# One product for two sets of group averages, and channel statistics taken earlier, in a fused two-layer image kernel

## The chip, the cores and the metric

The kernel runs on one core of a Trainium2 chip. The metric is the device time of one execution in microseconds (us); the time stated is the median of several executions. The core has TensorE (matrix products, called PE in the profile), VectorE (DVE), ScalarE (ACT), GpSimd (POOL), and SyncE (SP), whose queue issues the DMA transfers. Each engine executes its own instructions in order and waits at semaphores for the others.

## What is computed

The input x holds 32 images of 128 channels and 56x56 pixels. Two layers follow each other, each on a group-normalised input (32 groups of 4 channels) and each added to what went in:

```python
x = x + _L0_conv_ref(_gn(x), ...)   # channel gate: mean per channel -> 3-tap conv with
                                    # fractional offsets -> sigmoid -> x * gate
x = x + _L1_conv_ref(_gn(x), ...)   # key/query/value projections, softmax over 3x3
                                    # neighbours at distances 1, 2 and 4, 1x1 conv out

def _gn(v, G=32, eps=1e-05):
    g = v.reshape(B_, G, C_ // G, H_, W_)
    m = jnp.mean(g, axis=(2, 3, 4), keepdims=True)
    s = jnp.var(g, axis=(2, 3, 4), keepdims=True)
    return ((g - m) / jnp.sqrt(s + eps)).reshape(v.shape)
```

The statistics of the second normalisation follow from those of the first and the gate, so each image is measured once, per channel, and group averages over 4 channels are needed twice: of the channel moments of x (ahead of the gate) and of those of the gated image (behind the gate).

## The kernel before

Channels lie on the 128 partitions. All engines run the same loop: for each image n and each of 25 **slots** t (a slot is one tile of 128 queries of image n), each does its share. A slot lasts 1.2 to 2.4 us, an image 44.73 us. In one slot TensorE computes, in this order: the scores of tile t (`scores`, L473), the transposes of tile t-3 (`transposed`, L487), in some slots the hidden layer of a strip (`hidden`, L527) or value products (`values`, L553), the context of tile t-5 (`context`, L508 and L513), in some slots the second layer of the strip one slot behind (`query_and_key`, L534), and last a product of the chain of statistics (`chain`).

VectorE in a slot: `masked` (L1036, reads the scores and finds their extreme), `reciprocals` and `scaled` for tile t-1 (L1044, L1053 or L1050), then `chain` (statistics L1092 and small steps), then `final` (L1061) or `values` (L1074). ScalarE: copies transposed tiles (L667), `exponentials` of tile t (L652), which wait for VectorE's `masked` of the same tile, and, except for strips 0 and 3, `hidden` (L675) only behind the exponentials; then keys (L697) and queries (L686). TensorE's `query_and_key` waits for `hidden` of ScalarE (semaphore `h_done`). Slots of hidden layers are `G_SLOT`; strip 4 has its hidden layer in slot 5 and its L534 in slot 6.

The **chain** of an image m (the gate and both normalisations) runs ahead of the image, at places given in the table `CH` and counted from two images ahead: place 25+t is slot t of image m-1, place t is slot t of image m-2. It has these steps: `STATS`: seven `bn_stats` (L1092), one for each seventh of the image; `aggr`: `bn_aggr` into `of_x` (L1097); `p1`: one small GpSimd step (L811); `c1`: TensorE's product with `group_avg` into the bank `ps_v`, 6 columns (L569); `d1`: VectorE copies them out to `in_x` and squares them (L1100, L1101); `p3` to `p7` with `c3`: the gate; `c4`: a second product with `group_avg`, of the gated moments `of_x1`, 6 columns (L576); `d9`: copy to `in_x1` and squares (L1136, L1137); `p11`, `pw`, `c6`, `d13`: scaled weights and bias for the image.

The bank `ps_v` is also where the value products of seven column blocks go (`V_SLOT`, slots 4, 7, 10, 17, 18, 21 and 24). So `values` on TensorE waits (semaphore `dg`, table `CHAIN_READS`) until VectorE has copied out what the chain left there. `c4` stands at place 28, at the end of slot 3; the next value product is in slot 4.

In the order of every queue the tables alone decide: nothing is rescheduled at run time. The load of image n+3 (`LOAD`) stands in slot 19.

Of the kernel before, what the change touches and what calls it, by code (L numbers as in the profile page):

```python
# [19 lines left out]
GN = 4  # L20
# [34 lines left out]
CH = dict(aggr=12, p1=12, c1=13, d1=14, p3=15, c3=19, d4=20, a4=21, p4=21, d6=25,  # L55
          a6=25, d7=26, p7=26, c4=28, d9=28, p11=31, pw=32, c6=36, d13=37)
# [141 lines left out]
def build(nc, x, par, w1, w2, wv, wo, bo, bv, wg, out):  # L198
    with ExitStack() as ctx:
# [66 lines left out]
        of_x = sb("of_x", [P, 2 + GN])  # L266
        of_x1 = sb("of_x1", [P, 2 + GN])
        in_x = sb("in_x", [P, 2 + GN])
        in_x1 = sb("in_x1", [P, 2 + GN])
# [111 lines left out]
        def images(first, last, drain=0, register=None):  # L381

            with nc.Block() as block:
# [73 lines left out]
                def _(pe):  # L457
# [79 lines left out]
                    def values(m, b):  # L537
# [19 lines left out]
                    def chain(m, at):  # L557
                        if at in (ch(m)["c1"], ch(m)["c3"], ch(m)["c4"], ch(m)["c6"]):
# [650 lines left out]
```

## Time and profile before

| | us |
|---|---|
| median of 3 runs | 1479.59 |
| lowest, highest | 1479.5, 1479.63 |
| profiled execution | 1480.63 |
| its span | 1478.9 |

| engine | busy us | share of the span |
|---|---|---|
| PE | 1445.5 | 98% |
| PE weight loads | 1180.4 | 80% |
| DVE | 1256.4 | 85% |
| ACT | 1169.7 | 79% |
| POOL | 914.7 | 62% |

All times of rows are from this one execution, counted from the start of its span. Ends of matmuls are modelled, so the distance from one start to the next is the better measure of what an instruction costs. A fp32 product is listed as two (x2). The mean granted clock of TensorE is 0.997.

### The profile page before, as it was taken

The numbers are of one execution on the slowest core, as the hardware profiler recorded it, in microseconds if no ns is written. First come the engines' busy times: TensorE is split into PE (matmuls) and PEld (weight loads), VectorE is DVE, ScalarE is ACT, GpSimd is POOL, SyncE is SP. The second block draws the span as 40 slices with busy tenths as digits, with TensorE's granted clock in tenths as the row PEclk, the third lists the DMA queues.
The fourth block names the chain that finished last, engine by engine and source line by source line (L and its number), as shares of the span: only waits on it lengthen the run. The fifth ranks groups of instructions, "written<-read, shape, count | busy, mean of one in ns | idle before, by whom it ended". The sixth has DMA issues, their size and how long they took to land.

```text
span 1478.9 us, 34970 instructions
## 1 busy us (share of the span) xinstructions
PE 1445.5 (98%) x9123; PEld 1180.4 (80%) x9123; DVE 1256.4 (85%) x4602; ACT 1169.7 (79%) x3047; POOL 914.7 (62%) x2049
## 2 busy tenths in 40 slices
PE   5899999999999999999999999999999999999998
PEld 2688888888888888888888888888888888888886
DVE  7788888888888888888888888888888888888876
ACT  3688888788878788778788778888878888787886
POOL 5766566576666575665675665665665765665730
PEclk9999999999999999999999999999999999999999
DMA  3334554445554345554345554445544455544344
GB/s 137 86 95 151 171 154 127 119 144 154 161 163 127 110 144 163 155 166 117 113 148 167 155 156 109 128 151 170 155 127 122 140 154 164 161 127 112 101 117 145
DMA packets 104706, 205.95 MB, mean 139 GB/s; under 512 B 13632, under 2 KB 83776, under 8 KB 96448
## 3 DMA queue, kind: packets, MB, share of 16 engines
q1 hardware_dynamic: 103632, 203.49, 46.4%
q8 instruction: 79, 1.29, 0.4%
q14 instruction: 115, 0.94, 0.2%
q10 hardware_dynamic: 880, 0.23, 0.1%
HBM read 51.62 MB, written 51.38 MB: 70 GB/s over the span
## 4 chain that ended last, share of the span: by engine, by line
PE 96%; issue 1%; POOL 1%; ACT 0%; DVE 0%; ACTq 0%; POOLq 0%; DVEq 0%
PE ps_s L473 24%; PE ps_o L508 20%; PE ps_v L553 12%; PE ps_t L487 12%; PE ps_p L527 11%; PE ps_p L534 11%; PE ps_o L513 3%; PE ps_v L573 0%; PE ps_v L576 0%; PE ps_v L569 0%; PE ps_v L580 0%; PE ps_t L534 0%; ACT qq L686 0%; POOL hats L831 0%; ACT hid L675 0%
## 5 line engine op out<-in xcount | busy, mean ns | idle before, releaser
L652 ACT ACTIVATE e<-e,zmin 128x256 f32<-128x256 f32 x800 | 403.1, 504 | 154.4 <-DVE zmin L1036 150.6
L1036 DVE CUSTOM_DVE_ANT_0 e<-ps_s,mask 128x256 f32<-128x256 f32 x800 | 337.3, 422 | 146.8 <-PE ps_s L473 138.6
L508 PEld LDWEIGHTS ps_o<-eT,v 128*128 128x128 f32 x2688 | 380.3, 191 | 82.9 <-issue 70.2
L508 PE MATMUL ps_o<-eT,v 128*128 128x128 f32 x2688 | 430.3, 275 | 0.4 <-ACT eT L667 0.3
L473 PE MATMUL ps_s<-kk,qq 128*128 128x256 f32 x1408 | 427.6, 386 | 1.7 <-DVE zmin L1036 1.7
L897 POOL TENSOR_SCALAR xb<-raw,g 128x32 f32<-128x32 f32 (+3 forms) x768 | 353.8, 476 | 0.0
L487 PE MATMUL ps_t<-ident,e 128*128 128x128 f32 x1600 | 305.7, 273 | 0.0
L487 PEld LDWEIGHTS ps_t<-ident,e 128*128 128x128 f32 x1600 | 225.2, 141 | 80.5 <-issue 0.2
L667 ACT ACTIVATE eT<-ps_t 128x512 f32<-128x512 f32 (+1 forms) x416 | 236.8, 569 | 63.9 <-PE ps_t L487 60.5
L1053 DVE SCALAR_TENSOR_TENSOR e<-e,rz,keep 128x256 f32<-128x256 f32 x480 | 254.6, 530 | 17.1
L473 PEld LDWEIGHTS ps_s<-kk,qq 128*128 128x128 f32 x1408 | 223.6, 192 | 49.0 <-issue 40.5
L553 PE MATMUL ps_v<-wvoT,xb 128*128 128x128 f32 x1580 | 214.7, 276 | 3.8 <-issue 0.2
L527 PE MATMUL ps_p<-raw,w1x 128*128 128x448 f32 x448 | 207.7, 545 | 1.1 <-ACT hid L675 0.7
L534 PE MATMUL ps_p<-hid,w2T 128*128 128x448 f32 x442 | 203.9, 543 | 1.8 <-ACT hid L675 1.8
L553 PEld LDWEIGHTS ps_v<-wvoT,xb 128*128 128x128 f32 x1580 | 193.8, 192 | 10.4 <-issue 10.4
L686 ACT ACTIVATE qq<-ps_p,bn_t 64x192 f32<-64x192 f32 x442 | 195.0, 441 | 7.6
L870 POOL TENSOR_SCALAR raw<-raw,g 128x448 f32<-128x448 f32 x224 | 175.8, 789 | 33.2 <-PE ps_p L527 33.2
L697 ACT ACTIVATE kk<-ps_p,bn_t 64x448 f32<-64x448 f32 x221 | 139.5, 631 | 36.0 <-PE ps_p L534 23.5
L652 ACT ACTIVATION_READ_ACCUMULATOR e<-e,zmin 128x1 f32 x800 | 150.9, 189 | 0.0
L675 ACT ACTIVATE hid<-ps_p,b1x 128x448 f32<-128x448 f32 x224 | 140.5, 627 | 12.3 <-PE ps_p L527 8.8
L1050 DVE TENSOR_SCALAR e<-e,rz 128x256 f32<-128x256 f32 x320 | 134.1, 419 | 11.4
L1061 DVE TENSOR_TENSOR raw<-raw,ps_o 128x448 f32<-128x448 f32 x224 | 137.6, 614 | 3.8 <-PE ps_o L513 1.7
(150 smaller groups left out, 1550.9 us busy)
## 6 DMA issues: line engine op xcount, KB each, us to landing
out_dram<-raw SPq DMA_DIRECT2D x32, 1568.0 KB, 5.7
raw<-in_x_dram SPq DMA_DIRECT2D x31, 1568.0 KB, 6.6
v<-v SPq DMA_DIRECT2D x192, 224.0 KB, 2.9
kk<-kk SPq DMA_DIRECT2D x192, 112.0 KB, 2.2
ksp<-kk SPq DMA_DIRECT2D x192, 64.0 KB, 2.1
v<-v_last SPq DMA_DIRECT2D x64, 128.0 KB, 2.9
kk<-kk SPq DMA_DIRECT2D x32, 224.0 KB, 2.9
v<-v_last SPq DMA_DIRECT2D x64, 96.0 KB, 2.7
```

The lines of the kernel that those rows point to most:

```text
L473: nc.tensor.matmul(ps_s[i][:, 0:KEYS].rearrange("p (s h k) -> p h s k", s=2, h=2), qq[:, t, :], window.rearrange("p h (s k) -> p h s k", s=2),
L487: last = nc.tensor.transpose(o[:, base:base + KEYS].rearrange("p (a s k) -> p s a k", a=2, s=2)[:, i], e[:, t % RING, P * i:P * (i + 1)], ...
L508: last = nc.tensor.matmul(o[:, UPIX * (u - 1):UPIX * (u + 1)], v[:, s, u, :], eT[:, UPIX * (base + 2 * u - 1):UPIX * (base + 2 * u + 1)], ...
L527: nc.tensor.matmul(ps_p[:, 0:SPIX].rearrange("p (r c) -> p r c", c=SIDE), w1x[:, m.parity(), :], strip_of(m, g), start=True, stop=True).th ...
L534: nc.tensor.matmul(qk_bank(m, g)[:, 0:SPIX], w2T[:], hid[:], start=True, stop=True).then_inc(qk_ps.next(), 1)
L553: last = nc.tensor.matmul(v_bank(m, b)[:, P * j:P * (j + 1)], pixels, wvoT[:], start=True, stop=True)
L652: nc.scalar.activation(e[:, i, :], e[:, i, :], ACT.Exp, bias=zmin[:, i:i + 1], scale=-1.0, accum_out=zs[:, i:i + 1]).then_inc(e_done.next( ...
L667: nc.scalar.activation(eT[:, base:base + size], ps_t[(EPAIRS * n.parity() + j) % 2][:, 0:size], ACT.Copy).then_inc(eT_done.next(), 1)
L686: last = nc.scalar.activation(qq[HD * b:HD * (b + 1), at:at + len(units), UPIX * b:UPIX * (b + 1)], src[:, units[0]:UNITS:2, :], ACT.Relu, ...
L897: last = gp.tensor_scalar(to[:, k, rs, cs], src, col(Y_A + m.parity()), col(Y_B + m.parity()), ALU.mult, ALU.add)
L1036: nc.vector.tensor_tensor_reduce(e[:, i, :], ps_s[(TILES * n.parity() + t) % 2][:, 0:KEYS], mask[:].rearrange("p s h a b -> p (s h a b)"), ...
L1053: nc.vector.scalar_tensor_tensor(e[:, i, :], e[:, i, :], rz[:, i:i + 1], keep[:, KINDS.index(outside(t)), :], ALU.mult, ALU.mult).then_inc ...
```

## The change

For images 2 to 31 the product `c1` is gone. The moments of image m+1 ahead of its gate and those of image m behind its gate lie side by side in one buffer (`moments`), and `c4` of image m multiplies all 12 columns at once; one copy brings all 12 out (`averages`), and two squaring steps follow, one for each image. Images 0 and 1 (`alone`) keep a `c1` of their own. Since the moments of image m+1 must be ready by then, its statistics come earlier: `STATS` goes from slots 22 | 2, 4, 6, 8, 10, 11 to slots 22, 23, 24 | 0, 2, 3, 4, `aggr` and `p1` from slot 12 to slot 5. `c4` and `d9` go from place 28 (slot 3) to place 31 (slot 6), `p11` from 31 to 33, `pw` from 32 to 34. `LOAD` goes from 19 to 18.

```diff
-CH = dict(aggr=12, p1=12, c1=13, d1=14, p3=15, c3=19, d4=20, a4=21, p4=21, d6=25,
-          a6=25, d7=26, p7=26, c4=28, d9=28, p11=31, pw=32, c6=36, d13=37)
+CH = dict(aggr=5, p1=5, c1=6, d1=6, p3=15, c3=19, d4=20, a4=21, p4=21, d6=25,
+          a6=25, d7=26, p7=26, c4=31, d9=31, p11=33, pw=34, c6=36, d13=37)
...
-STATS = {-3: (0,), 2: (1,), 4: (2,), 6: (3,), 8: (4,), 10: (5,), 11: (6,)}
-
-LOAD = 19
+STATS_0 = {-3: (0,), 2: (1,), 4: (2,), 6: (3,), 8: (4,), 10: (5,), 11: (6,)}
+STATS = {-3: (0,), -2: (1,), -1: (2,), 0: (3,), 2: (4,), 3: (5,), 4: (6,)}
+
+LOAD = 18
...
-CHAIN_READS = ((2, "d1"), (4, "d4"), (13, "d9"), (15, "d13"))
-N_DG, N_PG, N_CG, N_AG = 15, 32, 4, 4
+CHAIN_READS = ((1, "d4"), (10, "d9"), (12, "d13"))
+N_DG, N_PG, N_CG, N_AG = 12, 31, 2, 4
+MOMENTS = 6
...
+def alone(m):
+
+    return m.offset < 2
...
+        def columns(m):
+
+            return 2 * MOMENTS if (m + 1).exists() and not alone(m + 1) else MOMENTS
...
-                        if at == ch(m)["c1"]:
+                        if at == ch(m)["c1"] and alone(m):
...
                         if at == ch(m)["c4"]:
-                            pe.wait_ge(pg.sem, pg.count(m, 21))
-                            nc.tensor.matmul(ps_v[:, 0:2 + GN], group_avg[:], of_x1[:], start=True,
-                                             stop=True).then_inc(cg.next(), 1)
+                            pe.wait_ge(pg.sem, pg.count(m, 20))
+                            if columns(m) > MOMENTS:
+                                pe.wait_ge(da.sem, da.count(m + 1, 1))
+                                pe.wait_ge(pa.sem, pa.count(m + 1, 1))
+                            nc.tensor.matmul(ps_v[:, 0:columns(m)], group_avg[:], moments[:, m.parity(), 0:columns(m)],
+                                             start=True, stop=True).then_inc(cm.next(), 1)
...
                         if at == ch(m)["d9"]:
-                            dve.wait_ge(cg.sem, cg.count(m, 3))
-                            step(13, nc.vector.tensor_copy(in_x1[:], ps_v[:, 0:2 + GN]))
-                            step(14, nc.vector.scalar_tensor_tensor(squares[:], moment(in_x1, APART, GN), 1.0,
-                                                                    moment(in_x1, APART, GN), ALU.mult, ALU.mult,
+                            dve.wait_ge(cm.sem, cm.count(m, 1))
+                            step(10, nc.vector.tensor_copy(averages[:, m.parity(), 0:columns(m)], ps_v[:, 0:columns(m)]))
+                            step(11, nc.vector.scalar_tensor_tensor(squares[:], moment(in_x1(m), APART, GN), 1.0,
+                                                                    moment(in_x1(m), APART, GN), ALU.mult, ALU.mult,
                                                                     accum_out=col(SQ1)))
+                            if columns(m) > MOMENTS:
+                                square_x(m + 1, 2)
```

How rows move, at three places. In these listings an instruction stands with its line, its tiles (`g` is a table of single columns, `ps_...` are PSUM banks) and the semaphores that it waits for; lines of the changed kernel are some 30 higher.

**TensorE, end of slot 3 and slot 4.** Before, from the context products of slot 3 to the value products of slot 4:

```order
L508 MATMUL ps_o<-eT,v 128x128 [waits eT_done]
L508 MATMUL ps_o<-eT,v 128x128
L576 MATMUL ps_v<-of_x,group_avg 128x6 [waits pg,v_done]
L473 MATMUL ps_s<-kk,qq 128x2x2x64 [waits q_done,z_done,k_copied1,k_copied0]
L487 MATMUL ps_t<-ident,e 128x2x64 [waits n_done]
L487 MATMUL ps_t<-ident,e 128x2x64
L553 MATMUL ps_v<-wvoT,xb 128x128 [waits dg,xb_done,v_done]
L553 MATMUL ps_v<-wvoT,xb 128x128 x3
```

Now, the same stretch:

```order
L535 MATMUL ps_o<-eT,v 128x128 [waits eT_done]
L535 MATMUL ps_o<-eT,v 128x128
L500 MATMUL ps_s<-kk,qq 128x2x2x64 [waits q_done,z_done,k_copied1,k_copied0]
L514 MATMUL ps_t<-ident,e 128x2x64 [waits n_done]
L514 MATMUL ps_t<-ident,e 128x2x64
L582 MATMUL ps_v<-wvoT,xb 128x128 [waits dg,xb_done,v_done]
L582 MATMUL ps_v<-wvoT,xb 128x128 x3
```

The 6-column product that stood between slot 3 and the scores of slot 4 is gone, and the value product L553 (now L582) no longer has a chain product shortly ahead of it.

**TensorE, end of slot 6 and slot 7.** Before, from the context products of slot 6 to the value products of slot 7:

```order
L508 MATMUL ps_o<-eT,v 128x128 [waits eT_done]
L508 MATMUL ps_o<-eT,v 128x128
L534 MATMUL ps_p<-hid,w2T 128x448 [waits h_done]
L473 MATMUL ps_s<-kk,qq 128x2x2x64 [waits q_done,z_done,k_copied0,k_copied1]
L487 MATMUL ps_t<-ident,e 128x2x64 [waits eT_done,n_done]
L487 MATMUL ps_t<-ident,e 128x2x64
L553 MATMUL ps_v<-wvoT,xb 128x128 [waits dg,xb_done,v_done]
```

Now, the same stretch:

```order
L535 MATMUL ps_o<-eT,v 128x128 [waits eT_done]
L535 MATMUL ps_o<-eT,v 128x128
L561 MATMUL ps_p<-hid,w2T 128x448 [waits h_done]
L610 MATMUL ps_v<-moments,group_avg 128x12 [waits da,pa,pg,v_done]
L500 MATMUL ps_s<-kk,qq 128x2x2x64 [waits q_done,z_done,k_copied0,k_copied1]
L514 MATMUL ps_t<-ident,e 128x2x64 [waits eT_done,n_done]
L514 MATMUL ps_t<-ident,e 128x2x64
L582 MATMUL ps_v<-wvoT,xb 128x128 [waits dg,xb_done,v_done]
```

The 12-column product stands now behind L534 (now L561) of slot 6, ahead of the value product of slot 7, and waits for the moments of the next image too (`da`, `pa`).

**VectorE, slots 2 to 4** (`ISA e,zmin` is `masked`). Before, from `scaled` in slot 2 to `masked` in slot 4:

```order
L1053 SCALAR_TENSOR_TENSOR e<-e,rz,keep 128x256 [waits rz_done]
L1092 BN_STATS stats<-raw 128x6
L1036 ISA e,zmin<-ps_s,mask 128x256 [waits e_done,t_done,s_done]
L1036 ISA zmin 128x1
L1044 RECIPROCAL rz<-zs 128x1 [waits e_done]
L1053 SCALAR_TENSOR_TENSOR e<-e,rz,keep 128x256 [waits rz_done]
L1136 COPY in_x<-ps_v 128x6 [waits cg]
L1137 SCALAR_TENSOR_TENSOR squares,g<-in_x 128x4 [waits dg]
L1036 ISA e,zmin<-ps_s,mask 128x256 [waits t_done,e_done,s_done,dg]
```

Now, the same engine from `scaled` in slot 3 to `values` in slot 4:

```order
L1087 SCALAR_TENSOR_TENSOR e<-e,rz,keep 128x256 [waits rz_done]
L1133 BN_STATS stats<-raw 128x6
L1070 ISA e,zmin<-ps_s,mask 128x256 [waits e_done,t_done,s_done]
L1070 ISA zmin 128x1
L1078 RECIPROCAL rz<-zs 128x1 [waits e_done]
L1087 SCALAR_TENSOR_TENSOR e<-e,rz,keep 128x256 [waits rz_done]
L1133 BN_STATS stats<-raw 128x6
L1108 TENSOR_TENSOR v<-ps_v,wobv 128x512 [waits c_done,v_ps]
```

The copy and the squares are gone from slot 3, and a `bn_stats` (now L1133) stands there; the copy with its two squares is in slot 6 now. In slots 23, 24 and 0, which these rows don't show, one `bn_stats` each is new in the same way, and the ones of slots 6, 8, 10 and 11 are gone. The order of ScalarE's instructions and that of SyncE's transfers are the same in both kernels: between slots 18 and 19 SyncE has nothing else.

## Rows read from the trace of the kernel before

**Rows 1.** The page: busy time by engine, and the chain that ended last.

```profile
PE 1445.5 (98%) x9123; PEld 1180.4 (80%) x9123; DVE 1256.4 (85%) x4602; ACT 1169.7 (79%) x3047; POOL 914.7 (62%) x2049
...
PE 96%; issue 1%; POOL 1%; ACT 0%; DVE 0%; ACTq 0%; POOLq 0%; DVEq 0%
```

**Rows 2.** Timeline of TensorE, slot 13 twice; columns: start us, length us, instruction, count.

```profile
696.80 0.28 PE L569 MATMUL ps_v<-of_x,group_avg 128*128 128x6 f32 x2
...
741.53 0.28 PE L569 MATMUL ps_v<-of_x,group_avg 128*128 128x6 f32 x2
...
742.19 0.38 PE L487 MATMUL ps_t<-ident,e 128*128 128x128 f32 x2
```

**Rows 3.** Timeline of TensorE: value products of slot 17, and slots 3 and 4.

```profile
702.59 1.06 PE L553 MATMUL ps_v<-wvoT,xb 128*128 128x128 f32 x8
...
722.98 0.28 PE L576 MATMUL ps_v<-of_x,group_avg 128*128 128x6 f32 x2
...
723.64 0.38 PE L487 MATMUL ps_t<-ident,e 128*128 128x128 f32 x2
724.15 1.13 PE L553 MATMUL ps_v<-wvoT,xb 128*128 128x128 f32 x8
```

**Rows 4.** Waits over the whole span: us in total, times, longest us.

```profile
PEld ps_v L553 <- issue: 10.4, 32, 0.4
```

**Rows 5.** Timeline of VectorE, slot 23 to the start of slot 5, same image.

```profile
714.10 0.42 DVE L1036 CUSTOM_DVE_ANT_0 e<-ps_s,mask 128x256 f32<-128x256 f32 x1 [0.28 <-PE ps_s L473]
...
715.95 0.42 DVE L1036 CUSTOM_DVE_ANT_0 e<-ps_s,mask 128x256 f32<-128x256 f32 x1 [0.29 <-PE ps_s L473]
...
717.72 0.42 DVE L1036 CUSTOM_DVE_ANT_0 e<-ps_s,mask 128x256 f32<-128x256 f32 x1 [0.27 <-PE ps_s L473]
...
718.26 0.70 DVE L1053 SCALAR_TENSOR_TENSOR e<-e,rz,keep 128x256 f32<-128x256 f32 x1
...
721.62 0.48 DVE L1053 SCALAR_TENSOR_TENSOR e<-e,rz,keep 128x256 f32<-128x256 f32 x1
722.02 0.62 DVE L1092 BATCH_NORM_STATS2 stats<-raw 128x6 f32<-128x448 f32 x1
722.55 0.41 DVE L1036 CUSTOM_DVE_ANT_0 e<-ps_s,mask 128x256 f32<-128x256 f32 x1
...
723.08 0.74 DVE L1053 SCALAR_TENSOR_TENSOR e<-e,rz,keep 128x256 f32<-128x256 f32 x1
723.75 0.15 DVE L1136 COPY in_x<-ps_v 128x6 f32<-128x6 f32 x1
...
724.47 0.42 DVE L1036 CUSTOM_DVE_ANT_0 e<-ps_s,mask 128x256 f32<-128x256 f32 x1
...
726.54 0.42 DVE L1036 CUSTOM_DVE_ANT_0 e<-ps_s,mask 128x256 f32<-128x256 f32 x1
```

**Rows 6.** Timeline of ScalarE, slot 5.

```profile
727.00 0.51 ACT L652 ACTIVATE e<-e,zmin 128x256 f32<-128x256 f32 x1 [1.36 <-DVE zmin L1036]
...
727.50 0.61 ACT L675 ACTIVATE hid<-ps_p,b1x 128x448 f32<-128x448 f32 x1
```

**Rows 7.** Timeline of TensorE, slot 6.

```profile
727.19 0.60 PE L473 MATMUL ps_s<-kk,qq 128*128 128x256 f32 x2
727.62 0.38 PE L487 MATMUL ps_t<-ident,e 128*128 128x128 f32 x2
727.84 0.61 PE L508 MATMUL ps_o<-eT,v 128*128 128x128 f32 x4
728.29 0.92 PE L534 MATMUL ps_p<-hid,w2T 128*128 128x448 f32 x2
```

**Rows 8.** Timelines of ScalarE and TensorE, same pair of lines, slot 6 of image 0.

```profile
55.61 0.61 ACT L675 ACTIVATE hid<-ps_p,b1x 128x448 f32<-128x448 f32 x1
...
56.28 1.02 PE L534 MATMUL ps_p<-hid,w2T 128*128 128x448 f32 x2 [0.43 <-ACT hid L675]
```

**Rows 9.** Timeline of GpSimd, slots 2 and 3.

```profile
722.84 1.58 POOL L870 TENSOR_SCALAR raw<-raw,g 128x448 f32<-128x448 f32 x2
```

More of the change, by code:

```diff
@@ L265, in build @@
         spread_s = sb("spread_s", [P, GN])
[L266 to L269, printed above, removed]
+        moments = sb("moments", [P, 2, 2 * MOMENTS])
+        averages = sb("averages", [P, 2, 2 * MOMENTS])
         squares = sb("squares", [P, GN])
@@ L307, in build, with of_x1, of_x, in_x1 @@
         N_BAND = N_IOTA + 3 + 4
+        def of_x1(m):
+            return moments[:, m.parity(), 0:MOMENTS]
+        def of_x(m):
+            return moments[:, (m + 1).parity(), MOMENTS:2 * MOMENTS]
+        def in_x1(m):
+            return averages[:, m.parity(), 0:MOMENTS]
+        def in_x(m):
+            return averages[:, (m + 1).parity(), MOMENTS:2 * MOMENTS]
+        def columns(m):
+            return 2 * MOMENTS if (m + 1).exists() and not alone(m + 1) else MOMENTS
         def qk_bank(m, g):
@@ L548, in values @@
                                 pe.wait_ge(dg.sem, dg.count(m + 1, max(held, default=0)))
+                                if alone(m + 1) and ch(m + 1)["d1"] <= V_SLOT[b] + TILES:
+                                    pe.wait_ge(da.sem, da.count(m + 1, 2))
                             held = [k for k, at in CHAIN_READS if ch(m)[at] <= V_SLOT[b] + 2 * TILES]
@@ L557, in chain @@
                     def chain(m, at):
-                        if at in (ch(m)["c1"], ch(m)["c3"], ch(m)["c4"], ch(m)["c6"]):
+                        if at in (ch(m)["c3"], ch(m)["c4"], ch(m)["c6"]) or at == ch(m)["c1"] and alone(m):
                             banks = sum(v_at <= at - TILES for v_at in V_SLOT)
@@ L584, in tables @@
                     def tables(t):
[L585 removed]
+                        if t == FIRST["c1"] + 1:
                             pe.wait_ge(g_const, N_ID)
@@ L903, in slot @@
                             chain(m, at)
-                        if n.offset == first + 1 and t == CH["p3"] + 1:
+                        if n.offset == first + 1 and t == FIRST["p3"] + 1:
                             borders()
@@ L1076, in values, with square_x @@
                                                 ALU.add).then_inc(v_done.next(), 1)
+                    def square_x(m, counts):
+                        nc.vector.scalar_tensor_tensor(squares[:], moment(in_x(m), APART, GN), 1.0,
+                                                       moment(in_x(m), APART, GN), ALU.mult, ALU.mult,
+                                                       accum_out=col(SQ)).then_inc(da.next(counts), counts)
+                        dve.wait_ge(da.sem, da.count(m, 3))
                     def chain(m, at):
@@ L1082, in step @@
                             dve.wait_ge(dg.sem, dg.count(m, k))
-                        for u in (STATS_1 if m.offset == 1 else STATS).get(at, ()):
+                        for u in {0: STATS_0, 1: STATS_1}.get(m.offset, STATS).get(at, ()):
                             if u == (2 * (PIECES - 1) if m.offset == 0 else 0):
@@ L1095, in chain @@
                             dve.wait_ge(bs_done.sem, bs_done.count(m, UNITS))
[L1096 to L1106 removed]
+                            nc.vector.bn_aggr(moment(of_x(m), MEAN, 2), stats[:].rearrange("p a b -> p (a b)")
+                                              ).then_inc(da.next(), 1)
+                        if at == ch(m)["d1"] and alone(m):
+                            dve.wait_ge(c_alone, m.offset + 1)
+                            nc.vector.tensor_copy(in_x(m), ps_v[:, 0:MOMENTS]).then_inc(da.next(), 1)
+                            dve.wait_ge(da.sem, da.count(m, 2))
+                            square_x(m, 1)
+                        if at == ch(m)["d4"]:
+                            dve.wait_ge(cg.sem, cg.count(m, 1))
+                            step(1, nc.vector.tensor_copy(pooled_row[:], ps_v[:, 8:8 + P]))
                             dve.wait_ge(ag.sem, ag.count(m + -1, 3))
```

123 lines of the change are left out of this document (58 added, 65 removed).

## The prediction

> **What bounds the kernel now.** The page first: TensorE is busy 98% of the span and carries 96% of the chain that ended last [rows 1]. So nothing counts that doesn't take work from TensorE or make it wait. The next view is TensorE's timeline over one image in the middle. The product c1 of two successive images starts at 696.80 and 741.53 [rows 2]: an image takes 44.73 us. In it I went from each product's start to the next, looking for a distance above what the same kind costs elsewhere, and found one. The transposes of a slot cost 0.22 us (727.62 to 727.84) [rows 7], but from those of slot 4 (723.64) to the value products (724.15) it is 0.51 [rows 3]: a gap of 0.29 us. It recurs in every image: the loads of weights ahead of L553 sat idle 32 times for 10.4 us in all [rows 4]. VectorE's timeline shows why. The value products wait until d9 has copied the averages out of the shared bank, and the copy starts at 723.75 only, because the `scaled` ahead of it took 0.74 us [rows 5].
>
> Third, how close is each other wait of TensorE to being late? The closest is L534 of slot 6. It waits for `hidden` on ScalarE, which stands behind the exponentials of slot 5, which wait for `masked` of slot 5 on VectorE. These start at 726.54, 727.00 and 727.50 [rows 5, 6], L534 at 728.29 [rows 7]. Where L534 was seen waiting for that line, it started 0.67 us after `hidden` did (55.61 to 56.28) [rows 8]. So it could have started at 727.50 + 0.67 = 728.17: 0.12 us to spare. That is what I watch for any delay of VectorE.
>
> **What is taken from TensorE.** From c1's start to the next transposes it is 0.66 us (741.53 to 742.19), for the scores alone 0.43 (727.19 to 727.62) [rows 2, 7]: c1 costs 0.23 us. The widened c4 costs what it did: four products of 128 columns are listed at 1.06 in slot 17, 0.27 each, and c4 with 6 columns at 0.28 [rows 3], so 6 columns more are 0.00, at most 0.01. It leaves slot 3 and comes back in slot 6, behind L534. The gap of 0.29 goes, since no product of the chain stands ahead of slot 4's value products any more, and with it the slower start behind a wait: L553 is listed at 1.13 there and at 1.06 in slot 17, 0.07 us [rows 3]. If nothing became late, each image would gain 0.23 + 0.29 + 0.07 = 0.59 us, and 30 images 17.7 us.
>
> **What is added to VectorE ahead of slot 5.** From slot 23 to slot 4 VectorE had one `bn_stats` in slot 2 and one in slot 4; now it has them in 23, 24, 0, 2, 3 and 4, four more. Each takes 0.53 us from its start to the next start (722.02 to 722.55): + 2.12 us. The copy and the square of slot 3 go, 723.75 to 724.47: - 0.72. Before, `masked` of slot 5 began 726.54 - 714.10 = 12.44 us after that of slot 23, and in these 12.44 us VectorE waited only twice, 0.29 and 0.27 us, ahead of slots 24 and 0. An instruction with a follower right behind it gives way 0.08 us earlier than listed (0.62 against those 0.53 or 0.54), so the slack is 0.29 + 0.27 + 0.16 = 0.72 us, and it is used up: - 0.72. One more term: `scaled` took 0.70 us in slot 0 (718.26) and 0.74 in slot 3 (723.08), against 0.48 in slot 2 (721.62) [rows 5]. The one of slot 3 began 0.24 us into a step L870 of GpSimd [rows 9]. In slot 0 VectorE will be some 0.3 us later than GpSimd, past most of such a step, so - 0.22. In slot 3 I keep the long one, since GpSimd's two L870 stand behind a reciprocal of VectorE in slot 1 and are as late as VectorE itself. The sum: 12.44 + 2.12 - 0.72 - 0.72 - 0.22 = 12.90 us. Nothing changes for TensorE and VectorE before slot 23, so `masked` of slot 5 begins at 714.10 + 12.90 = 727.00 in place of 726.54.
>
> **What is late next.** L534 of slot 6 can start at 727.00 + 0.96 (726.54 to 727.50) + 0.67 = 728.63. TensorE would be ready for it at 728.29 - 0.59 = 727.70, as c4, the gap and the slow start are gone ahead of it. It waits 0.93 us, and behind a wait L534 is listed at 1.02 in place of 0.92: another 0.10 [rows 7, 8]. Behind L534 stands c4 (0.23) now, where c1 (0.23) was further on, which cancels. An image gets longer by 728.63 + 0.10 - 728.29 = **0.44 us**: a gain of 0.59 is paid for with 1.03.
>
> **Other terms, each with its cover.** c4 waits for GpSimd's p1 of the next image, which follows `bn_aggr` in VectorE's slot 5, about 1.2 us after `masked` of that slot; TensorE comes to c4 2.4 us after it, since it stands behind the same VectorE: 0. The value products of slot 7 wait for d9 again. VectorE will be through with `scaled` of slot 6 and wait for c4. It can begin the copy some 0.40 behind c4's start and TensorE can go on 0.40 behind the copy's start (723.75 to 724.15 [rows 3, 5]), 0.80 in all; TensorE gets there 0.88 behind c4 (0.66 and the transposes' 0.22 [rows 2, 7]). So 0, with 0.08 to spare. The second square stands behind the copy, where slots 8, 10 and 11 have lost their statistics, and can't cost more than the 0.72 that copy and square took together. Keys and queries on ScalarE come 0.6 us later in slots 2 and 3, about 0.2 us before slot 5's hidden layer needs them: 0. GpSimd's p11 and pw come two slots later, two slots before their readers. The order of transfers and of ScalarE is the same: 0.
>
> **The sum.** 29 images x 0.44 = 12.8 us. The next to last image has no statistics to take ahead and only gains, - 0.37, and once c1 goes with no c4 behind L534 in its place, - 0.23. At the start VectorE also gets more to do; I take 0, within 1 us either way. The span becomes 1478.9 + 12.2 = 1491.1 us. The profiled execution took 1480.63 around a span of 1478.9, and the median of the runs is 1479.59, 0.69 above the span. By the median the forecast is **1491.8 us**.
>
> **Its own bounds.** If `scaled` of slot 3 meets no step of GpSimd, 0.26 less per image: 1484.3 us. If those of slots 0 and 4 meet one too, 0.22 each: 0.44 more per image, 1504.6 us.
>
> **Rival 1: VectorE keeps up, and the kernel is faster.** All of 17.7 us comes: 1461.9 us. For this `masked` of slot 5 must begin at 727.70 - 0.96 - 0.67 = 726.07 or earlier, 0.93 before my value. For it speaks VectorE's 85% on the page, that is, 15% idle; against it, that of this idle time only 0.72 us lie between slots 23 and 5. Chance 0.10. **Rival 2: gain and wait cancel**, which an error of 0.44 us in those 12.90 would do: 1479.6 us. Chance 0.09.
>
> **Rival 3: GpSimd's steps shut VectorE out for longer.** In slot 3 `scaled` began within the first L870 (722.84; two in 1.58, so the first ended at 723.63), and VectorE's next instruction began at 723.75, 0.12 behind that end [rows 5, 9]. If instead `scaled` ran whole behind GpSimd's step, 0.40 (722.02 less 721.62), slot 3 would take 0.28 more: 0.28 x 29 = 8 us, 1499.9 us. The condition is that VectorE's later place meets GpSimd's steps less luckily than in the rows. The Trainium skill (SBUF — State Buffer, section "SBUF: two separate sides") states as a rule that GpSimd and a VectorE instruction with two SBUF inputs contend for one pair of ports, that the first gets it for its whole instruction, and that the other fully blocks. By that rule the time would be this rival's; the rows agree that something is held back until L870 ends, but show 0.12 and not 0.40 behind it. Chance 0.14.
>
> **Rival 4: the second copy is late too.** If in slot 7 VectorE is busy when c4 is done, the value products lose there what they lost in slot 4, 0.29 + 0.07 per image, 10.4 us: 1502.2 us. It decides at 0.08 us of delay. Against it: by the sum VectorE is through with `scaled` of slot 6 some 0.3 us before c4's result. Chance 0.12.
>
> **How the numbers follow.** Forecast 0.55, rivals 0.10, 0.09, 0.14 and 0.12. The range of eight in ten leaves out rivals 1 and 2 and the far end of the bounds: 1483 to 1506. A change of 0.2% (3 us) is about the least that can be told from none. Faster by more than that 0.11, within it 0.10, slower by more 0.79.
>
> **What would show it.** Right: in the trace after, TensorE has no gap ahead of the value products of slot 4 and one near 0.93 us ahead of L561 (the old L534) in slot 6, ended by ScalarE's `hidden`; ScalarE's exponentials of slot 5 wait for VectorE; VectorE has no idle time from slot 23 to slot 5; an image takes 45.17 us. Wrong: no gap in slot 6 and an image of 44.14 us (rival 1, and with it the sum on VectorE), a `scaled` of 1 us in slot 3 (rival 3), a second gap ahead of the value products of slot 7 (rival 4).

## The result, and the profile after

| | before | after |
|---|---|---|
| median of 4 runs each, us | 1479.61 | 1495.26 |
| lowest, highest | 1479.5, 1480.65 | 1494.73, 1495.92 |
| profiled execution, us | 1480.63 | 1494.73 |
| its span | 1478.9 | 1493.0 |

The ratio of the times is 1.0101, with a 95% interval of 1.0089 to 1.0113: the change costs 1%, 15.65 us by the medians and 14.1 us by the two profiled executions. The mean granted clock of TensorE is 0.996 (0.997 before). Forecast were +12.2 us and 1491.8 us.

The page of the changed kernel, first the busy times, then the chain that ended last; VectorE has entered it with 2%, ScalarE with 2% [rows 1 has both at 0%]:

```profile
PE 1440.2 (96%) x9063; PEld 1175.4 (79%) x9063; DVE 1234.3 (83%) x4572; ACT 1167.1 (78%) x3047; POOL 918.2 (62%) x2049
...
PE 92%; ACT 2%; DVE 2%; issue 1%; DMA 1%; POOL 0%; SPq 0%; ACTq 0%; DVEq 0%; POOLq 0%
```

Waits of TensorE and of its weight loads over the span (us in total, times, longest). There is one new wait, at strip 4's second layer, once in nearly every image; first its row before, then after. The loads ahead of the value products are down from 10.4 us in 32 times [rows 4] to 0.4 in 2.

```profile
PE ps_p L534 <- ACT hid L675: 1.8, 2, 1.3
```

```profile
PE ps_p L561 <- ACT hid L709: 23.4, 31, 1.0
...
PEld ps_v L582 <- issue: 0.4, 2, 0.2
```

TensorE's timeline from slot 4 to slot 7, which answers to [rows 3] and [rows 7]:

```profile
687.13 0.38 PE L514 MATMUL ps_t<-ident,e 128*128 128x128 f32 x2
687.34 1.06 PE L582 MATMUL ps_v<-wvoT,xb 128*128 128x128 f32 x8
...
690.96 0.61 PE L535 MATMUL ps_o<-eT,v 128*128 128x128 f32 x4
692.37 1.02 PE L561 MATMUL ps_p<-hid,w2T 128*128 128x448 f32 x2 [0.80 <-ACT hid L709]
693.22 0.29 PE L610 MATMUL ps_v<-moments,group_avg 128*128 128x12 f32 x2
693.36 0.68 PE L500 MATMUL ps_s<-kk,qq 128*128 128x256 f32 x2
693.88 0.38 PE L514 MATMUL ps_t<-ident,e 128*128 128x128 f32 x2
694.10 0.83 PE L582 MATMUL ps_v<-wvoT,xb 128*128 128x128 f32 x6
```

From the transposes of slot 4 to the value products it is 0.21 us, where it was 0.51. L561 follows the context products by 1.41 us where L534 followed them by 0.45 (727.84 to 728.29): 0.96 of waiting. The value products of slot 7 come 0.88 behind L610, with no gap.

VectorE's timeline, the same image, answers to [rows 5]; ScalarE's to [rows 6]:

```profile
677.81 0.42 DVE L1070 CUSTOM_DVE_ANT_0 e<-ps_s,mask 128x256 f32<-128x256 f32 x1 [0.28 <-PE ps_s L500]
...
682.28 0.48 DVE L1087 SCALAR_TENSOR_TENSOR e<-e,rz,keep 128x256 f32<-128x256 f32 x1
...
687.40 0.74 DVE L1087 SCALAR_TENSOR_TENSOR e<-e,rz,keep 128x256 f32<-128x256 f32 x1
688.07 0.61 DVE L1133 BATCH_NORM_STATS2 stats<-raw 128x6 f32<-128x448 f32 x1
...
689.12 0.57 DVE L1087 SCALAR_TENSOR_TENSOR e<-e,rz,keep 128x256 f32<-128x256 f32 x1
...
690.75 0.41 DVE L1070 CUSTOM_DVE_ANT_0 e<-ps_s,mask 128x256 f32<-128x256 f32 x1
...
693.55 0.17 DVE L1176 COPY averages<-ps_v 128x12 f32<-128x12 f32 x1 [0.39 <-PE ps_v L610]
```

```profile
691.20 0.51 ACT L686 ACTIVATE e<-e,zmin 128x256 f32<-128x256 f32 x1 [1.24 <-DVE zmin L1070]
...
691.70 0.61 ACT L709 ACTIVATE hid<-ps_p,b1x 128x448 f32<-128x448 f32 x1
```

`masked` of slot 5 starts 690.75 - 677.81 = 12.94 us after that of slot 23, and the rest of the chain follows as before: exponentials 0.45, hidden layer 0.50, L561 0.67 us later. Between these two no wait of VectorE is listed. From one L561 of slot 6 to the next it is 45.10 or 45.11 us in most images, where before it was 44.72 or 44.73: +0.38.

**Where the 14.1 us are.** I followed that one product of slot 6 through both traces:

| stretch, to the product of slot 6 | before | after | difference |
|---|---|---|---|
| start of the span to image 0 | 56.28 | 58.15 | +1.87 |
| image 0 to 1 | 45.87 | 46.52 | +0.65 |
| image 1 to 29, 28 intervals | 1252.31 | 1264.35 | +12.04 |
| 29 to 30 | 44.71 | 44.15 | -0.56 |
| 30 to 31 | 43.59 | 43.85 | +0.26 |
| 31 to the end of the span | 36.14 | 35.98 | -0.16 |

Of the 12.04, 28 x 0.38 = 10.6 are the regular images and 1.4 a few irregular ones, the longest 45.82 and 45.70. Image 1 is regular too: its L561 waits 0.80 us, as in the images behind it. So 0.38 of the 0.65 is the ordinary growth of an image, 29 x 0.38 = 11.0 in all, and the start proper costs 1.87 + 0.27 = 2.1 us.

### The profile page after: what moved, and what is told of

It is laid out like the page before. It is cut to its first block, busy times and chain, and to the rows that moved or that the text cites. A ratio compares the mean times of both kernels' runs of the same rounds, so it can differ in the third digit from the quotient of the medians.

```text
span 1493.0 us, 34698 instructions
## 1 busy us (share of the span) xinstructions
PE 1440.2 (96%) x9063; PEld 1175.4 (79%) x9063; DVE 1234.3 (83%) x4572; ACT 1167.1 (78%) x3047; POOL 918.2 (62%) x2049
## 4 chain that ended last, share of the span: by engine, by line
PE 92%; ACT 2%; DVE 2%; issue 1%; DMA 1%; POOL 0%; SPq 0%; ACTq 0%; DVEq 0%; POOLq 0%
PE ps_s L500 23%; PE ps_o L535 19%; PE ps_v L582 12%; PE ps_p L561 11%; PE ps_t L514 11%; PE ps_p L554 11%; PE ps_o L540 3%; ACT hid L709 1%; DMA ksp<-kk 1%; DVE stats L1133 1%; PE ps_v L604 0%; ACT e L686 0%; DVE e L1070 0%; DVE v L1108 0%; PE ps_s L637 0%
## 5 line engine op out<-in xcount | busy, mean ns | idle before, releaser
L931 POOL TENSOR_SCALAR xb<-raw,g 128x32 f32<-128x32 f32 (+3 forms) x768 | 362.0, 486 | 0.0
L1087 DVE SCALAR_TENSOR_TENSOR e<-e,rz,keep 128x256 f32<-128x256 f32 x480 | 243.2, 507 | 17.1
L561 PE MATMUL ps_p<-hid,w2T 128*128 128x448 f32 x442 | 207.0, 550 | 23.4 <-ACT hid L709 23.4
L582 PE MATMUL ps_v<-wvoT,xb 128*128 128x128 f32 x1580 | 213.4, 276 | 0.0
L582 PEld LDWEIGHTS ps_v<-wvoT,xb 128*128 128x128 f32 x1580 | 194.4, 192 | 0.4 <-issue 0.4
L864 POOL TENSOR_SCALAR hats<-hats 128x128 f32<-128x128 f32 x93 | 32.8, 353 | 249.0 <-ACT hats L757 243.5
L904 POOL TENSOR_SCALAR raw<-raw,g 128x448 f32<-128x448 f32 x224 | 166.9, 750 | 29.8 <-PE ps_p L554 29.6
L1084 DVE TENSOR_SCALAR e<-e,rz 128x256 f32<-128x256 f32 x320 | 140.0, 438 | 11.4
```

What stands on the lines that cost most here:

```text
L561: nc.tensor.matmul(qk_bank(m, g)[:, 0:SPIX], w2T[:], hid[:], start=True, stop=True).then_inc(qk_ps.next(), 1)
L582: last = nc.tensor.matmul(v_bank(m, b)[:, P * j:P * (j + 1)], pixels, wvoT[:], start=True, stop=True)
L931: last = gp.tensor_scalar(to[:, k, rs, cs], src, col(Y_A + m.parity()), col(Y_B + m.parity()), ALU.mult, ALU.add)
L1087: nc.vector.scalar_tensor_tensor(e[:, i, :], e[:, i, :], rz[:, i:i + 1], keep[:, KINDS.index(outside(t)), :], ALU.mult, ALU.mult).then_inc ...
```

## The experiments

Each kernel's time stands against runs of the kernel before on the same chip (1479.6 to 1480.8 us). "An image" is the distance that most images have in the trace. The three theories on trial: that VectorE's four more `bn_stats` ahead of slot 5 make strip 4's hidden layer late (mine); that c4's wait for the next image's moments holds TensorE; that what was taken off TensorE was worth less than I summed.

**e1: the hidden layer of strip 4 ahead of the exponentials, in the changed kernel.**

```diff
-RELU_FIRST = (0, 3)
+RELU_FIRST = (0, 3, 4)
```

> The changed kernel, with one more entry in ScalarE's table of strips whose hidden layer comes ahead of the slot's exponentials: strip 4 (slot 5). Theory (the statistics make VectorE late, and the lateness reaches TensorE only through the exponentials ahead of strip 4's hidden layer): the gap of 0.8 us ahead of L561 in slot 6 goes, an image takes 44.14 instead of 45.11 us, 29 images x 0.96 = 28 us less: 1467 us. Rival (the loss comes from c4 in its new place, from GpSimd or from transfers): 1490 us or more, since none of these is touched.

Measured 1479.97 us (10 runs), ratio to before 0.9995 [0.9985, 1.0004]; an image 44.56 us. The wait of L561 is gone, and with it 15 us. But the 1467 us were missed, and the rival's 1490 too: another wait had stood behind it. Timelines of e1, TensorE, VectorE, GpSimd:

```profile
686.00 0.92 PE L561 MATMUL ps_p<-hid,w2T 128*128 128x448 f32 x2
687.03 0.36 PE L610 MATMUL ps_v<-moments,group_avg 128*128 128x12 f32 x2
...
688.08 0.91 PE L582 MATMUL ps_v<-wvoT,xb 128*128 128x128 f32 x6
```

```profile
686.14 0.34 DVE L1137 BATCH_NORM_AGGREGATE moments<-stats 128x2 f32<-128x42 f32 x1
```

```profile
686.58 0.31 POOL L845 TENSOR_SCALAR moments<-spread_s,moments 128x4 f32<-128x4 f32 x1 [1.74 <-DVE moments L1137]
```

L610 starts 1.03 behind L561, where 0.75 is what that product takes without a wait (e3, below: 678.59 to 679.34): 0.28 late for `bn_aggr` and p1. It runs slowly behind the wait, and the value products of slot 7 are late too (688.08, 1.05 behind L610 in place of 0.88). So the second theory holds as well, but only once the first wait is out of the way. Five images took 45.04 to 45.30 us; in each a product waits for a transfer of keys, 3 us in all.

**e2: the same edit in the kernel before.**

> The same entry in the kernel before. Theory: there that wait had 0.12 us to spare and was never late, so nothing comes of it: 1479.6 us, within 1 us. Rival (the order on ScalarE is worth something by itself): 1470 us or less, and then e1 says little about the statistics.

1480.41 us, 1.0002 [0.9992, 1.0011]: nothing, as expected. e1's gain is a wait undone, not a better order as such.

**e3: the kernel before with only c4 moved**, from slot 3 to slot 6, behind L534, and with it the steps that read its result.

```diff
-a6=25, d7=26, p7=26, c4=28, d9=28, p11=31, pw=32, c6=36, d13=37)
+a6=25, d7=26, p7=26, c4=31, d9=31, p11=33, pw=34, c6=36, d13=37)
...
```

> The kernel before with c4, d9, p11 and pw at the places of the changed kernel (31, 31, 33, 34), c1 kept, the statistics where they were. Theory: the gap ahead of slot 4's value products and the slow start behind it go, 0.36 us x 30 images = 10.8 us less, 1468.8 us; no gap ahead of L534, since VectorE loses 0.72 us ahead of slot 5 and gains nothing. Rival (c4 behind L534 makes slot 7's value products wait as they did in slot 4): 1479.6 us.

1470.21 us, 0.9926 [0.991, 0.9943]; an image 44.35 us, -0.37. TensorE's timeline of e3, slots 6 and 7:

```profile
678.59 0.92 PE L534 MATMUL ps_p<-hid,w2T 128*128 128x448 f32 x2
679.34 0.28 PE L576 MATMUL ps_v<-of_x,group_avg 128*128 128x6 f32 x2
679.48 0.68 PE L473 MATMUL ps_s<-kk,qq 128*128 128x256 f32 x2
680.00 0.38 PE L487 MATMUL ps_t<-ident,e 128*128 128x128 f32 x2
680.22 0.83 PE L553 MATMUL ps_v<-wvoT,xb 128*128 128x128 f32 x6
```

That is the gap of 0.29 and the slow start of 0.07, as summed, and the value products of slot 7 don't wait (0.88 behind c4). One part of the change is a gain by itself.

**e4: the kernel before with only the statistics moved** to the changed kernel's slots.

> The kernel before with only the statistics moved to slots 22, 23, 24, 0, 2, 3 and 4 (bn_aggr stays in slot 12, both products and all else as before). Theory: masked of slot 5 comes 12.44 + 2.12 - 0.72 = 13.84 us behind that of slot 23, or 0.22 less, since slot 3 keeps its copy and squares; L534 then starts 1.06 to 1.28 us later and costs 0.10 more, 1.16 to 1.38 us per image x 29 = 34 to 40 us more, plus 1 to 2 at the start: 1514 to 1521 us. Rival (statistics may stand anywhere, VectorE is 15% idle): 1479.6 us.

1514.65 us, 1.0231 [1.0216, 1.0247], an image 45.83 us, 1.11 more than before, just under the 1.16 to 1.38 expected. TensorE waits at both places where it depends on VectorE:

```profile
PE ps_v L554 <- DVE in_x L1137: 16.0, 29, 0.6
...
PE ps_p L535 <- ACT hid L676: 8.5, 31, 1.3
```

The statistics alone cost 34 us; the rest of the change, c4 and d9 moved and c1 gone, gives 19 of them back.

**e5: the changed kernel with four statistics at half size** (`bn_stats` 1, 2, 3 and 5 of images 2 to 31 read 224 columns; the variances are those of part of the image).

```diff
-nc.vector.bn_stats(stats[:, u, :], raw[:, m.offset % RAWS, first:first + BATCH]
+size = BATCH // 2 if m.offset > 1 and u in (1, 2, 3, 5) else BATCH
+nc.vector.bn_stats(stats[:, u, :], raw[:, m.offset % RAWS, first:first + size]
```

> The changed kernel, but the four statistics of slots 23, 24, 0 and 3 read 224 columns in place of 448 (so the statistics of images from the third on are of part of their columns). Nothing else changes on any engine. Theory (VectorE's load ahead of slot 5 is the cause): each is 0.23 us shorter; two of them then fit into the waits that VectorE had ahead of slots 24 and 0, so masked of slot 5 comes 0.6 to 0.8 us earlier, the wait ahead of L561 falls from 0.97 to 0.15 to 0.35 us, an image takes 44.3 to 44.5 us: 1472 to 1478 us. Rival (not VectorE's load, but c4 and what surrounds it): 1495 us.

1475.03 us, 0.9966 [0.9953, 0.9978], an image 44.45 us; the wait of L561 for `hid` is down from 23.4 us to 6.1. It follows VectorE's time.

**e7: e1 and e5 together.**

> e1 and e5 together: hidden of strip 4 first, and four statistics of half the columns. In e1 a gap of 0.28 us ahead of c4 and one of 0.10 ahead of slot 7's value products were left. Theory (c4 waits there for bn_aggr and p1, which are late with VectorE): with VectorE 0.6 us earlier both go, an image takes 44.14 us against 44.56 in e1, 12 us less than e1: 1467 to 1469 us. Rival (c4 waits for something of its own, such as GpSimd's order): as e1, 1480 us.

1463.45 us, 0.9885 [0.987, 0.99], under the 1467 to 1469 expected; an image 44.03 us, and neither L561 nor L610 waits in the middle of the run. This is what an image costs TensorE, and it is 0.70 under 44.73, while I had summed 0.59. The rest is a gap of before that I had not seen (its timeline, slot 15):

```profile
743.29 0.38 PE L487 MATMUL ps_t<-ident,e 128*128 128x128 f32 x2
743.54 0.99 PE L527 MATMUL ps_p<-raw,w1x 128*128 128x448 f32 x2
744.36 0.39 PE L508 MATMUL ps_o<-eT,v 128*128 128x128 f32 x2
```

The hidden layer's product starts 0.25 behind the transposes in place of 0.22 and takes 0.82 to the next start in place of 0.75: 0.03 and a slow start of 0.07, 0.10 us in each image. In e7 the same product starts 0.22 behind and takes 0.75. In the kernel before it starts 0.1 us behind the end of ScalarE's queries (742.54 + 0.90), which it must wait for. The gap stands in the four kernels that keep `bn_aggr` in slot 12 and `d1` in slot 14 (before, e2, e3, e4) and in none of the others. e8 has a product in slot 13 again and doesn't have it, so it isn't c1's time on TensorE; which of the other two makes the queries late no run separates. The third theory falls: what was taken away was worth more than I had said.

**e8: the changed kernel with a product of 6 columns put back into slot 13.**

```diff
+if at == 13 and not alone(m):
...
+    nc.tensor.matmul(ps_v[:, 200:206], group_avg[:], group_avg[:, 0:6], start=True, stop=True)
```

> The changed kernel with a product of 6 columns put back where c1 stood, at the end of slot 13, of tables into unused columns of ps_v; nobody reads it. It measures c1's price by itself. By the rows of before 0.23 us x 30 = 6.9 us more: 1502.2 us. Rival (so small a product hides in the weight loads of its neighbours): 1495.3 us.

1498.43 us, 1.0119 [1.0104, 1.0134] against the changed kernel's 1.0101: +3.2 us in place of +6.9. In the trace an image is 45.27 or 45.32, +0.16 to +0.22, and the product delays its successors by 0.23, of which part is taken back ahead of L561, which waits for VectorE anyway. Another 1.3 us of the difference are the slow images of the changed kernel (1.4 us, see above), of which e8's trace has next to none. The price of c1, 0.23, holds up to the next wait; that it holds for the whole time these runs can't show, as their intervals are as wide as the difference.

**e10: image 2 as before too**, its own c1 in slot 13 and its statistics in the old slots, images 3 to 31 as in the change.

```diff
-    return m.offset < 2
+    return m.offset < 3
...
+         2: dict(CH, aggr=12, p1=12, c1=13, d1=14)}
...
-{0: STATS_0, 1: STATS_1}.get(m.offset, STATS)
+{0: STATS_0, 1: STATS_1, 2: STATS_0}.get(m.offset, STATS)
```

> The changed kernel with image 2 as before too: its own c1 in slot 13 of image 1 and its statistics in the old slots; images 3 to 31 as in the change. Theory: the 2.5 us that the changed kernel loses in images 0 and 1 (its L561 of slot 6 of image 0 starts 1.9 us later than before, that of image 1 another 0.65) come from image 2's statistics, taken while VectorE is late at the start, and from c4 of image 1, which waits for p1 of image 2. Then these 2.5 us come back, less 0.23 for the c1: that line starts near 56.3 us in image 0 and 102.2 in image 1, and the whole time is 2 us under the changed kernel's, 1492 to 1494 us. Rival: the start is lost to something else (the order of first loads, LOAD in slot 18), and the first L561 of slot 6 stays near 58 us, 1495 us.

1493.74 us, 1.0087 [1.0072, 1.0102]. The product of slot 6 is at 56.70 in image 0 and 102.82 in image 1 (58.15 and 104.67 after, 56.28 and 102.15 before). So 1.85 of the 2.5 us come back: most of the start is image 2's statistics, taken in image 0 while TensorE waits for VectorE anyway, and c4 of image 1 that waits for p1 of image 2; the run doesn't separate the two. 0.67 us stay. By their size they are image 1's ordinary growth, 0.38 (its L561 waits 0.79 here too), and image 2's own c1, 0.23. What is left is less than two executions differ by over this stretch: e8, the same kernel up to there, has that product of image 0 at 57.71, the changed kernel at 58.15. So this result rests on the two traces; the whole times, 1.0087 and 1.0101, have overlapping intervals.

**Better places.** Three more kernels keep the one product of 12 columns and e1's order on ScalarE, and give the statistics more room by a later c4; a fourth, e11, takes e1's order away again.

e6, with c4 and d9 in slot 9:

```diff
-CH = dict(aggr=5, p1=5, c1=6, d1=6, p3=15, c3=19, d4=20, a4=21, p4=21, d6=25,
-          a6=25, d7=26, p7=26, c4=31, d9=31, p11=33, pw=34, c6=36, d13=37)
+CH = dict(aggr=8, p1=8, c1=6, d1=6, p3=15, c3=19, d4=20, a4=21, p4=21, d6=25,
+          a6=25, d7=26, p7=26, c4=34, d9=34, p11=35, pw=36, c6=38, d13=39)
...
-STATS = {-3: (0,), -2: (1,), -1: (2,), 0: (3,), 2: (4,), 3: (5,), 4: (6,)}
+STATS = {-3: (0,), 0: (1,), 2: (2,), 3: (3,), 5: (4,), 6: (5,), 8: (6,)}
...
```

> The changed kernel with strip 4's hidden layer ahead of the exponentials (as in e1), and c4 and d9 three slots later still, in slot 9 ahead of the value products of slot 10; so the statistics need to be ready only by slot 8 and stand in slots 22, 0, 2, 3, 5, 6 and 8, bn_aggr and p1 in slot 8, p11, pw, c6 and d13 at 35, 36, 38 and 39. Theory (both waits that e1 and the changed kernel show come from VectorE being late from statistics that lie close together): neither c4 nor L561 nor slot 10's value products wait, an image takes 44.14 us, 0.59 less than before, 1462 to 1465 us. Rival (one product for two sets can't be fed in time wherever it stands, GpSimd's p11 then being late for c6 and the blocks of slot 11): 1480 us or more.

1470.84 us, 0.9932 [0.9917, 0.9947]: no better than e3, and neither the theory's time nor the rival's. Most images take 44.37 to 44.48, some 0.4 more than in e7. TensorE loses it in three places: 0.10 at the hidden layer's product of slot 8 (see e9), 0.11 at the value products of slot 21 and 0.19 at the second layer's product of slot 23. The value products of slot 21 wait for the copy d4 of slot 20, behind a `scaled` (a TENSOR_SCALAR there) that takes 0.91 us where e7 has 0.35. That slot 23 is late from the same cause is argued, not shown. VectorE and GpSimd in e6:

```profile
969.68 0.91 DVE L1084 TENSOR_SCALAR e<-e,rz 128x256 f32<-128x256 f32 x1
970.51 0.27 DVE L1146 COPY pooled_row<-ps_v 128x128 f32<-128x128 f32 x1
```

```profile
967.72 2.72 POOL L931 TENSOR_SCALAR xb<-raw,g 128x32 f32<-128x32 f32 x6
```

`scaled` gives way only where GpSimd's run of six copies ends, 970.44. It began 0.24 us into the fifth of them (969.44 to 969.80) and stood through the whole sixth (969.79 to 970.45). The same two in e7:

```profile
965.03 0.35 DVE L1084 TENSOR_SCALAR e<-e,rz 128x256 f32<-128x256 f32 x1
```

```profile
958.52 2.83 POOL L931 TENSOR_SCALAR xb<-raw,g 128x32 f32<-128x32 f32 x6
```

There the run was over at 961.35, two slots before: a later c4 makes w1x late, and all copies behind it.

e9, with c4 in slot 8 (place 33, everything else of the chain one slot sooner than in e6), in two forms: a with statistics in slots 22 | 0, 2, 3, 5, 6, 7, b in 22, 23 | 0, 2, 3, 5, 6.

> The changed kernel with the hidden layer of strip 4 ahead of the exponentials on ScalarE, the 12-column product and its copy in slot 8 (place 33), bn_aggr and p1 in slot 7, and the statistics in slots 22, 0, 2, 3, 5, 6, 7. Slot 8 has no value products, and those of slot 10 come two slots behind the copy. In e6, with the product in slot 9, an image took 44.4 us in place of the 44.03 seen without a wait; the trace there shows VectorE's scaled of slot 20 at 0.91 us in place of 0.35, ending where a run of six edge copies of GpSimd (L931) ends, and the value products behind it late. Theory: the product in slot 9 made w1x and with it these copies late; one slot sooner they are 1.8 us earlier and miss that scaled: image 44.03 to 44.15 us, 1458 to 1464 us. Rival: some scaled is met all the same, image 44.3 to 44.5, 1467 to 1473 us.

> As e9_c4_33a, with the statistics in slots 22, 23, 0, 2, 3, 5, 6, so that bn_aggr has a slot without a bn_stats. Theory: the same as e9_c4_33a within 3 us, if VectorE has room in slot 23; rival: the bn_stats in slot 23 makes VectorE late at slot 5 again, with L561 waiting, and the image 0.1 to 0.5 us longer than in e9_c4_33a.

a: 1463.45 us, 0.9884 [0.987, 0.9899]; b: 1466.82 us, 0.9907 [0.989, 0.9923]. In a that `scaled` is 0.35 again, since the six copies end 0.40 before it; slot 18's is met instead (0.77), where nobody waits. Both lags of slots 21 and 23 are gone. VectorE and GpSimd of e9 a:

```profile
960.92 0.77 DVE L1087 SCALAR_TENSOR_TENSOR e<-e,rz,keep 128x256 f32<-128x256 f32 x1
...
964.76 0.35 DVE L1084 TENSOR_SCALAR e<-e,rz 128x256 f32<-128x256 f32 x1
```

```profile
961.39 2.97 POOL L931 TENSOR_SCALAR xb<-raw,g 128x32 f32<-128x32 f32 x6
```

An image takes 44.16 or 44.22 us, slightly over the 44.03 to 44.15 expected. All that is left above e7's 44.03 lies in one place, slot 8. There the hidden layer's product waits for ScalarE's queries of the strip before and starts slowly; TensorE and ScalarE of e9 a:

```profile
677.10 0.38 PE L514 MATMUL ps_t<-ident,e 128*128 128x128 f32 x2
677.40 1.02 PE L554 MATMUL ps_p<-raw,w1x 128*128 128x448 f32 x2
678.26 0.38 PE L535 MATMUL ps_o<-eT,v 128*128 128x128 f32 x2
```

```profile
676.46 0.90 ACT L720 ACTIVATE qq<-ps_p,bn_t 64x256 f32<-64x256 f32 x2
```

It starts 0.30 behind the transposes in place of 0.22 and takes 0.86 to the next start in place of 0.75. With c4 gone from slot 6 TensorE comes to it 0.22 us sooner than in e7: once more a wait that stood behind another one.

**Form a is the best full kernel of this study, 1.2% under the one before**, with the same work. In b most images take 44.14 to 44.21, so the `bn_stats` in slot 23 does no harm; its 3.4 us over a (within 3 was expected) lie in five images of 44.6 to 45.3, where TensorE waits for a transfer:

```profile
PE ps_s L500 <- DMA ksp<-kk: 2.7, 5, 0.8
```

e11, form a with strip 4's hidden layer behind the exponentials again:

> e9_c4_33a with the hidden layer of strip 4 behind the exponentials again, as in before and after. Theory: VectorE has one bn_stats more than before between slots 23 and 5 (0.53 us) and the copy and square less (0.72), so masked of slot 5 comes at most 0.2 us sooner than before, while TensorE comes to L561 of slot 6 0.69 us sooner; with 0.12 us to spare before it waits 0.4 us and starts slowly, 0.10: an image of 44.6 to 44.7 us, 1475 to 1479 us. Rival: moving the later statistics was enough and L561 doesn't wait, an image of 44.2 us, 1462 to 1465 us.

1471.17 us, 0.9933 [0.9916, 0.995], an image 44.42 or 44.49; L561 waits 0.1 to 0.2 us and starts slowly. Theory (1475 to 1479) and rival (1462 to 1465) were both missed. The direction is that of the theory, the size is not: I had taken 0.4 of waiting. From `masked` of slot 23 to that of slot 5 it is 12.32 us there, 0.12 less than before.

## Why the prediction was right, and where its sizes were off

**What bounds it, and what is late next: shown.** The gap of slot 4 went; L561 of slot 6 took its place as the wait, by the chain named: VectorE's `masked`, exponentials, hidden layer. 12.94 us between the two `masked` against 12.90 forecast; 1.62 us from `masked` to L561 against 1.63; 0.96 of waiting against 0.93. e1 (the wait taken away) and e5 (VectorE's work halved) moved the time as the chain says, and e4 shows that it is the statistics.

**The sum on VectorE: right in its parts, too.** `scaled` of slot 0 took 0.48, as assumed, that of slot 3 0.74, as assumed. That of slot 4 took 0.57 in place of 0.48, as it met one of GpSimd's small copies: slot 4 came out 0.08 longer than summed, the other slots 0.04 shorter in all.

**What is taken from TensorE: mis-sized**, 0.59 in place of 0.70 (e7). The step that failed is the search for distances above what the same kind costs elsewhere: the prediction names one and there are two. The second, in slot 15, is 0.10 in all. So an image grew by 0.38 and not by 0.44: over 29 images 1.7 us less than forecast.

**The start: "0 within 1 us" was wrong**, +2.1 beside image 1's ordinary growth. The term was put at nothing without a reason. Image 0 isn't like the others: TensorE waits for VectorE in it, and an argument from a middle image says nothing about that. The wait for ScalarE's hidden layer [rows 8] and one for GpSimd's chain were already in the trace of before. The last chain product of that stretch, behind slot 6 of image 0, waits twice as long now, and for another step: before for p7 of its own image (L848), now for p1 of image 2 (L845). First the row of before, then that of after:

```profile
57.84 0.36 PE L576 MATMUL ps_v<-of_x,group_avg 128*128 128x6 f32 x2 [0.54 <-POOL of_x L848]
```

```profile
60.30 0.36 PE L610 MATMUL ps_v<-moments,group_avg 128*128 128x12 f32 x2 [1.13 <-POOL moments L845]
```

e10 brings 1.85 back, and in it this product waits 0.53 us for p7 again.

**Transfers at 0: 1.4 us in a few images.** In the longest, TensorE waits for the copies of keys:

```profile
427.62 0.70 PE L500 MATMUL ps_s<-ksp,qq 128*128 128x256 f32 x2 [0.46 <-DMA ksp<-kk]
```

Weight loads waited 7.6 us for them, 1.4 before, and all four images of 45.25 us or more have such a wait. It comes and goes from trace to trace (0.7 in e9 a, 6.7 in e9 b, 2.1 in e8, which is nearly the changed kernel). With one trace of each kernel no run tells whether the arrangement or the execution sets it: it stays open.

**c4's wait at 0: right only behind the other wait.** I gave as cover that TensorE "stands behind the same VectorE", and so it does, as long as L561 waits. e1 took that wait away, and c4's cost 0.28 at once, about 0.5 per image with its slow start and the value products behind it. Had I priced the repair of my own wait, I would have promised 13 us too much, as I did for e1.

**The end** gave -0.46 (forecast -0.60). Then 14.1 us are 2.1 of the start, 11.0 of 29 regular images, 1.4 of transfers and -0.46, where the forecast had 0, 12.8, 0 and -0.60. So that the total came within 2 us of the forecast's 12.2 is in part luck: 1.7 us too much in the images made up for half of what the start and the transfers cost. The other 1.5 of the 15.65 are scatter of single executions: the profiled one of before was 1.0 over its median, that of after 0.5 under.

**The rivals.** VectorE did not keep up (rival 1). Gain and wait did not cancel in the changed kernel; in e1 the whole times did, by another wait (rival 2). Rival 3's long lock was not met: `scaled` of slot 3 takes 0.74 as before, and VectorE's next instruction starts at 688.07, 0.20 behind the end of the first of two GpSimd steps. The prediction had 0.12 for this in the kernel before, as it halved the two steps' 1.58 us; taken singly the first lasts 0.72 (722.84 to 723.56) and the second 0.88, so it was 0.19 there too, and rival 3's price was nearer 0.21 than 0.28 per image. The first step singly, before and after:

```profile
722.84 0.72 POOL L870 TENSOR_SCALAR raw<-raw,g 128x448 f32<-128x448 f32 x1
```

```profile
687.16 0.71 POOL L904 TENSOR_SCALAR raw<-raw,g 128x448 f32<-128x448 f32 x1
```

The Trainium skill (SBUF — State Buffer, section "SBUF: two separate sides") states that the second of two instructions on the shared ports fully blocks. In slot 3 of both kernels something was held back so, but VectorE's next instruction came 0.19 or 0.20 us behind the end of GpSimd's step and not 0.40; the same 0.20 stands in slot 4 of the changed kernel and in slot 18 of e9 a. In e6, where `scaled` is a TENSOR_SCALAR (0.27 to the next start when undisturbed), it was 0.06. So a blocked `scaled` is over sooner behind the lock than its own length. What it pays before is the rest of GpSimd's instruction in slot 3, but in e6 the rest of one copy and all of the next: no run tells when it gets in between two of GpSimd's instructions. Rival 4's second gap did not come: 0.88 us from c4 to the value products, as summed.

## What to carry to other kernels

A product saved on a full TensorE is worth only what the slot behind it can start sooner, so price the engine that has to deliver the inputs earlier, over the stretch in which they are due, not over the whole loop: VectorE was 15% idle over the span and had 0.72 us to spare in the 28% of an image that counted. Engines that execute in order hide waits behind one another; after removing one, look at what the same engine waits for next, or the gain is counted twice. When work has to be ready earlier for a merged step, try first to put the merged step later: here two slots later, with the statistics spread into the room that this gave and one step of ScalarE reordered, turned +1.0% into -1.2%.

## What the runs showed of the hardware

A product of 6 or 12 columns costs TensorE 0.23 us: 0.14 to the next start and another 0.09 in the row of another product, as the scores behind it take 0.52 in place of 0.43. The doubled columns cost at most 0.01 (listed 0.29 against 0.28).

A wait costs TensorE more than its length: the product behind one is longer by 0.07 to 0.10 us (1.02 against 0.92, 1.13 against 1.06, 0.36 against 0.29), even where the wait itself is 0.03 us. In the changed kernel L561 takes 0.86 to the next start behind a wait and 0.75 otherwise, almost without exception.

One instruction of VectorE can take 0.91 in place of 0.35 us when it meets GpSimd's small copies of 0.36 to 0.66 us each. From e6 to e9 a the run of copies moved by 1.4 us against that instruction (it began 1.96 us ahead of it, then 3.37), and this decided whether it was met, and whether anybody waited for it.
